# Rows of field 24 gathered by GpSimd instead of fetched by SyncE, and two more tiles a quad looked up on TensorE

## The reference

```
emb = tbl[idx]                                   # 2048 x 26 x 32
bi = emb[:, FIRST, :] * emb[:, SECOND, :]        # 2048 x 325 x 32
a = relu(bi @ att_w_w + att_w_b)                 # 8 hidden
weight = softmax(a @ att_d_w + att_d_b, axis=1)  # over the 325 pairs
out = sigmoid(concat([sum(weight * bi), dense]) @ fin_w + fin_b)
```

## Time and profile before

| | us |
|---|---|
| three runs | 478.12, 478.24, 480.02 |
| median | 478.24 |
| profiled execution, span (no other time of it is given) | 755.4 |
| busy: TensorE, VectorE, GpSimd, ScalarE | 489.4, 419.0, 343.8, 118.3 |

### The profile page before, as it was taken

The page is one execution under the profiler, slowest core; times in us unless marked ns, Lnnn a source line. Parts: engine busy times, 40 slices in busy tenths (PEclk is TensorE's granted clock), DMA queues, the critical chain, the costliest instruction groups (busy, mean ns, idle before and its releaser), DMA issues.

```text
span 755.4 us, 9968 instructions
## 1 busy us (share of the span) xinstructions
PE 489.4 (65%) x2788; PEld 175.7 (23%) x2788; DVE 419.0 (55%) x692; ACT 118.3 (16%) x218; POOL 343.8 (46%) x357
## 2 busy tenths in 40 slices
PE   2853102136686888737696898647687989999516
PEld 0321000012222233312232233212222224433102
DVE  6943003047475656444485666254476666899616
ACT  4211000003011123000011132000012132013114
POOL 6777777624745441744564541744564640000000
PEclk9985555559888899958898999868898999999958
DMA  7532521201211111111221110121221210000000
GB/s 234 120 18 13 99 13 12 13 3 9 13 8 12 8 10 33 12 8 10 11 11 10 10 10 4 13 37 9 11 12 9 12 10 2 2 2 2 0 1 1
DMA packets 15495, 15.60 MB, mean 21 GB/s; under 512 B 8177, under 2 KB 14161, under 8 KB 15057
## 3 DMA queue, kind: packets, MB, share of 16 engines
q0 software_dynamic: 11296, 5.81, 14.3%
q1 hardware_dynamic: 3488, 8.38, 3.1%
q10 hardware_dynamic: 656, 0.79, 0.4%
HBM read 14.93 MB, written 0.02 MB: 20 GB/s over the span
## 4 chain that ended last, share of the span: by engine, by line
SPq 59%; issue 38%; DVE 1%; PE 1%; DMA 1%; ACT 1%; ACTq 0%
SPq L411 51%; SPq L407 7%; DMA index<-look_index 0%; PE sums_s L515 0%; DVE ring L855 0%; PE sums_f L501 0%; PE first L491 0%; ACT score L685 0%; SPq L380 0%; DVE neg_max_early L891 0%; DMA emb_placed<-tables 0%; SPq L385 0%; ACT second_s L627 0%; ACT hidden L614 0%; PE back_s L538 0%
## 5 line engine op out<-in xcount | busy, mean ns | idle before, releaser
L441 POOL DMA_INDIRECT emb<-tables,rows x308 | 294.0, 955 | 261.0 <-DVE emb_t L831 164.6
L476 PE MATMUL looked_own<-look_parts,onehot 128*128 128x448 bf16 x735 | 178.8, 388 | 119.3 <-issue 75.3
L855 DVE TENSOR_TENSOR ring<-emb_t,turned 128x512 f32<-128x512 f32 (+9 forms) x180 | 193.9, 1114 | 3.4
L476 PE MATMUL back_s<-look_parts,onehot 128*128 128x448 bf16 x441 | 100.5, 380 | 73.2 <-issue 49.7
L614 ACT ACTIVATE hidden<-first,par 128x512 f32<-128x512 f32 (+1 forms) x84 | 56.4, 677 | 507.8 <-PE first L491 304.6
L476 PEld LDWEIGHTS looked_own<-look_parts,onehot 128*128 128x128 bf16 x735 | 72.7, 104 | 229.4 <-issue 158.9
L491 PE MATMUL first<-ring,par 128*32 128x512 f32 (+1 forms) x672 | 105.7, 616 | 22.6 <-DVE ring L855 8.2
L501 PE MATMUL sums_f<-ring,par 128*32 128x512 f32 (+1 forms) x672 | 105.7, 605 | 5.1 <-issue 4.2
L840 DVE TENSOR_TENSOR look_masked<-back_s,look_mask 128x448 f32<-128x448 f32 x21 | 13.0, 621 | 125.0 <-remote 70.8
L750 DVE TENSOR_TENSOR onehot<-chunk_of,turned 128x2048 bf16<-128x2048 f16 (+3 forms) x30 | 53.0, 1767 | 43.0 <-PE looked_own L476 26.4
L476 PEld LDWEIGHTS back_s<-look_parts,onehot 128*128 128x128 bf16 x441 | 43.6, 103 | 137.6 <-issue 79.8
(11 more groups left out here) (71 smaller groups left out, 145.0 us busy)
## 6 DMA issues: line engine op xcount, KB each, us to landing
emb_placed<-tables SPq DMA_DIRECT2D x896, 0.1 KB
emb<-tables,rows POOLq DMA_INDIRECT x308
ring<-tables SPq DMA_DIRECT2D x3, 1568.0 KB
chunk_of<-chunk_numbers SPq DMA_DIRECT2D x3, 512.0 KB, 3.6
ring<-tables SPq DMA_DIRECT2D x1, 896.0 KB
emb<-tables,rows_first POOLq DMA_INDIRECT x44
ring<-tables SPq DMA_DIRECT2D x1, 672.0 KB
chunk_of<-chunk_numbers ACTq DMA_DIRECT2D x1, 384.0 KB, 3.9
```

Of the source, the lines that this page charges most:

```text
L441: pool.indirect_dma_start(emb[:, f, g * D:(g + 1) * D], None, stacked, bass.IndirectOffsetOnAxis(ap=row, axis=0), element_offset=at,).then ...
L476: mm = nc.tensor.matmul(looked_rows[look_bank[tile]], onehot[:, c, g * P:(g + 1) * P], look_parts[:, n, c, k, :], start=c == 0 and k == 0, ...
L855: nc.vector.tensor_tensor(slot[:, at:at + n, :], emb_t[:, i:i + n, :], turned[:, f % 2, :].unsqueeze(1).broadcast_to((P, n, P)), ALU.mult) ...
```

## The change

SyncE fetches no rows of field 24 and `emb_placed`, the row numbers for it and the copies go. GpSimd gathers all four tiles of field 24. Of field 19 all four tiles are looked up on TensorE and none is gathered, so that 16 tiles of a quad (32 steps) are looked up; `STEP_FIELDS` has 30 entries for them. SyncE issues the table and chunk loads alone.

```diff
-LOOK_TILES = (4, 4, 4, 2)
+LOOK_TILES = (4, 4, 4, 4)
-STEP_FIELDS = (1, 2, 2, 3, 4, 4, 5, 6, 6, 7, 8, *range(8, 21), 22, 24)
+STEP_FIELDS = (1, 2, 2, 3, 4, 4, 5, 6, 6, 7, 8, 8, 9, 9, 10, 11, 11, 12, 13, 13, 14, 15, 15, 16, 17, 18, 19, 20, 22, 24)
...
         if f in LOOK:
             return G - LOOK_TILES[LOOK.index(f)]
-        return G - PLACED if f == SP_FIELD else G
+        return G
...
-            sp.wait_ge(sp_rows_ready, 1)
-            tiles = 0
-            for q in range(QUADS):
-                for i in range(PLACED - TILES_SP[q], PLACED):
...
-                        for k in range(ROWS_SP):
-                            sp.dma_start(emb_placed[p + k:p + k + 1, q, i * D:(i + 1) * D],
-                                         stacked[bass.ds(at[k], 1), :]).then_inc(sp_gathered[tiles], 16)
-                    tiles += 1
+            sp.wait_ge(look_low_made[0], len(STEPS))
+            load_table(2)
+            sp.wait_ge(chunk_numbers_home, 16)
+            load_chunks(1)
+            sp.wait_ge(look_low_made[1], len(STEPS))
+            load_table(3)
+            for q in range(2, QUADS):
+                load_chunks(q)
...
-                    if q == 0 and f == SP_FIRST:
-                        for n in range(QUADS):
-                            for i in range(PLACED - TILES_SP[n]):
...
-                for f in range(1, F):
-                    if f == SP_PLACE:
-                        place_rows()
+                for f in range(1, F):
...
-                    if f == SP_FIELD:
-                        dve.wait_ge(placed, q + 1)
```

More of the change, by code:

```diff
@@ L45, in layout, with attention_fm @@
     return cols, at
-def attention_fm(nc, dense, sparse, tables, params, look_index, sp_index, chunk_numbers, out):
+def attention_fm(nc, dense, sparse, tables, params, look_index, chunk_numbers, out):
     f32, i32, bf16 = mybir.dt.float32, mybir.dt.int32, mybir.dt.bfloat16
@@ L128, in gathers_of @@
             return G - LOOK_TILES[LOOK.index(f)]
-        return G - PLACED if f == SP_FIELD else G
-    PLACED_COLS = slice((G - PLACED) * D, G * D)
-    assert FIRST_FIELDS <= SP_FIRST < SP_PLACE < SP_FIELD and len(TILES_SP) == QUADS and max(TILES_SP) <= PLACED
-    assert SP_FIELD not in LOOK
+        return G
     assert G * D == P and B % (P * G) == 0 and RING < GROUPS and 1 < END_GROUPS
@@ L197, in attention_fm @@
         emb = sb("emb", [P, F, G * D])
-        emb_placed = sb("emb_placed", [P, QUADS, PLACED * D])
-        sp_ids = sb("sp_ids", [T, P], i32)
-        sp_rows = sb("sp_rows", [T, P], i32)
         look_parts = sb("look_parts", [P, LOOKS, CHUNKS, PARTS, CHUNK_ROWS * D], bf16)
@@ L234, in attention_fm @@
             final[0:QUADS * LOOKS * G].rearrange("p g e -> p (g e)")[:, G * P + i * P:G * P + (i + 1) * P] for i in range(3))
-        sp_clamped, sp_wrap = (score[0:T].rearrange("p g e -> p (g e)")[:, i * P:(i + 1) * P] for i in range(2))
         neg_max = sb("neg_max", [P, G])
@@ L278, in attention_fm @@
         rows_ready = sem("rows_ready")
[L279 to L284, removed]
         gathered = [sem(f"gathered{f}") for f in range(F)]
@@ L369, in _ @@
             sp.dma_start(index[:], look_index).then_inc(index_in, 16)
-            sp.dma_start(sp_ids[:], sp_index).then_inc(sp_ids_in, 16)
             stacked = tables.rearrange("f v d -> (f v) d")
@@ L727, in _ @@
             dve.wait_ge(par_in, 16)
[L730 to L737, removed]
             def make_onehots(of, n, part):
@@ L1008 @@
             by_block[:, list(LOOK)].reshape(P, -1, G, len(LOOK)).transpose(1, 3, 2, 0).reshape(-1, P)),
-        "sp_index": np.ascontiguousarray(by_block[:, SP_FIELD].reshape(P, -1).T),
     }
```

## The result

| | before | after |
|---|---|---|
| median of four runs, us | 478.58 | 505.68 |
| span of a profiled execution, us | 755.4 | 503.8 |
| busy: TensorE, VectorE, GpSimd, us | 489, 419, 344 | 457, 434, 346 |

The changed kernel is slower: ratio 1.0553, 95% interval 1.0527 to 1.0579, so 26.5 us (the medians of the table lie 27.1 apart); 499 (483 to 511) was forecast, with a chance of 0.82 for slower. The profiled execution of after took 505.6 us by the clock of the runs with a span of 503.8: what lies around the span is 1.8 us, not the 9 us of the sum.

What follows compares the result with a forecast made beforehand. Three paths (TensorE 461, SyncE 468, GpSimd 469 us) were taken to stand within 2%. After the change TensorE alone decides at 490, +21 us against 469; with 9 us around it 499 us, range 483 to 511.

Steps and rivals of the forecast that it cites:

- the 9 us of the sum: Runs against the longest path, 469 us: 9 us for what lies around the span and unseen stalls, kept for after.
- the free stretches: Parts of the stalled trace where engines run freely; adding these up gave a full quad of 107.8 us.
- SyncE's path: Kernel before: table loads, 28 batches of fetches at 15.6 us, last landing and the rest to the end, 468 us.
- GpSimd's on top, 469 us: Kernel before: 353 gathers, 1.2 us landing and 14.4 from field 25's turn to the end, the longest of three sums.
- Removing SyncE's fetches is worth nothing: Dropping 896 fetches and 28 row-number loads frees only the 468 us path; earlier table loads were taken as 0.
- The lookup's price: Eight more tiles of 21 matmuls on TensorE, 3.93 us each, 31.4 us; its path goes from 461 to 490.
- Full quad 107.8 + 7.9 = 115.7: A full quad on TensorE after the change: two more looked-up tiles add 7.9 us to 107.8.
- Quad 0 ends at 50.3 + 107.8: After the change, quad 0 ends at 158.1 us, counted from six tiles looked up at 50.3; before, 150.2.
- TensorE's path was 461 by my sum: Kernel before: quads 0 to 2 end at 365.8 us, quad 3 needs 73.4 + 21.4 more.
- quad 3's late fields: TensorE's pauses beside the late fields of quad 3 were to hide 2 us of the added 7.9.
- Rival A: TensorE decided already before the change, so all 29 us between 461 and 490 are seen: 507 us; chance 0.22.
- The reading by weight loads: Weight loads at 36% mean two thirds of TensorE may be free; the 31.4 us vanish, time stays near 477.

Runs made afterwards that it cites:

- e1: Kernel before, with each of SyncE's 7 tiles fetched by one DMA of 128 fixed rows instead of 128 single fetches: 479.13 us, ratio 1.0006.
- e14: Kernel before, SyncE's fetches kept, with 16 tiles a quad looked up, 345 gathers, and lookups without the low bf16 part: 469.77 us, ratio 0.9803.
- e6: Kernel before, each lookup leaving out the low bf16 part, 14 matmuls a tile instead of 21: 478.32 us, ratio 0.9981.
- e8: e1 with field 23 also brought by plain DMAs of fixed rows from SyncE, 337 gathers instead of 353: 470.24 us, ratio 0.9826 to the kernel before.
- e13: Kernel before, without splitting the tables of fields 15 and 19, same number of matmuls: 472.78 us, ratio 0.9872.
- e5: Changed kernel with SyncE's 896 single fetches kept, into a tile nobody reads: 504.48 us, ratio 1.0540 to the kernel before.
- e12: Changed kernel without splitting the tables of fields 15 and 19, same number of matmuls: 495.03 us, ratio 1.0340 to the kernel before.
- e16: Changed kernel with 15 tiles a quad looked up and a list with two steps beside fields 9 and 13, none beside 17 and 19: 510.0 us.
- e7: Changed kernel, each lookup leaving out the low bf16 part, 14 matmuls a tile instead of 21: 474.45 us, ratio 0.9906 to the kernel before.

## Why the prediction was right, and where its sizes were off

*Reading the stalled profile.* Right. Working only with the free stretches gave a quad of 107.8 us (106.6 and 105.8 in e1) and SyncE's path 468 (467.5 in e14).

*Which path decided before.* The sum had GpSimd's on top, 469 us. The experiments show the place (e6, e8, e13) and correct the size: 476.2 us of span in e1, which runs as long as the kernel before. Gathers land 3.4 us after their issue (e1) and not 1.2, the first 44 take 3 us longer than in the stalled trace (51.1 against 47.9), and the last field that waits for a gather is field 23, at 452.8; field 25 is turned at 461.8, behind field 24's own products, and not when its last gather lands. With the span that right, only 1.7 to 2.6 us lie around it in all the runs. The 9 us that I carried over as "around the span" were mostly this path.

*Removing SyncE's fetches is worth nothing.* Right: e1 1.0006, and e5 from the other side.

*The lookup's price.* Forecast 29 us on TensorE's path, measured 35.4 (e8 to after). The step that was off is "Full quad 107.8 + 7.9 = 115.7. Quad 0 ends at 50.3 + 107.8", in two ways. First the level of both paths: I gave quad 0 a full quad's length from the sixth tile on, 150 us before and 158 after, and it ends at 162.4 (e8) and 171.0, 12 to 13 us later. It left out what splitting two tables does to VectorE and TensorE there; e12 puts 10.7 us on that, and the other 2 stay open. Since full quads were 1 to 2 us shorter than I had them, TensorE's path was 461 by my sum and is 468.3 in e8; that of after was 490 and is 503.8. Then the growth: the quads grew by 8.6, 8.6, 9.3 and 9.0 us (e8 to after) and not by 7.9, 7.9, 7.9 and 5.9. Two tiles' matmuls are 7.9; in quads 1 and 2 the rest is pauses (TensorE is idle 3.4 us a quad and was 2.7), and quad 3's late fields hid nothing. That the list brings these pauses was not tried with 16 tiles; e16 shows that a list alone can be worth 13 us.

*The net.* 490 + 9 = 499 came out 6.7 us low: TensorE's path 14 us too short, what lies around it 7 us too long. The errors partly cancelled: that the forecast came this near is in part luck. Rival A's figure (507) came nearer, though its mechanism is wrong: TensorE did not decide before.

*The reading by weight loads*, which the prediction took from the Trainium skill (Perfetto Trace Analysis, Identifying the Most-Contended Engine). TensorE's weight loads are at 36% of the span after, as before in the earlier trace rows, while leaving out a third of the lookup's matmuls gave back 31 us (e7). The reading by which two thirds of the engine were free would have had the time at 477. Here the measurement goes against it: the spacing of the starts told the bound, and the share of weight loading didn't.

## What to carry to other kernels

Add up each engine's path separately from stretches in which it ran freely, and look at all of them: here three paths stood at 467.5 (SyncE, e14), 468.3 (TensorE, e8) and 476.2 us (GpSimd, e1) of span, and work moved from one that had a little room (SyncE) to one that had 8 us (TensorE) costs everything beyond these 8 us. Work that stands in one engine's queue by a list written out by hand has a price of its place as well as of its size; measure it with the list that goes with it. To find out whether an engine decides, take a good part of its work away and change nothing else.

## What the runs showed of the hardware

A profiled execution can be 58% longer than the runs (755.4 against 478.2 us) and show one matmul every 2.8 us with no wait that the profile names; a later profile of a kernel with the same fetches showed none of it. 896 DMAs of 128 bytes beside the gathers slowed nothing (e5). VectorE's subtractions of two SBUF operands held up gathers by some 6 us in all (e13 against e1); a gather beside one took up to 2.7 us instead of 0.94. A pause of 6.5 us on TensorE was followed by matmuls at the 1.2 GHz level (0.39 us each, granted clock 0.50 from 233.3 to 238.0 us, e16).
